# VectorE's dependent chains issued in turns, two products moved ahead, and v centred without an fp32 matmul, in a cross-attention and mixture-of-experts kernel

## The reference, cut to what matters

```python
x = x + xattn(layernorm(x), ctx, ctx, igate_w, igate_b, fgate_w, fgate_b, out_w)
x = x + ffn(layernorm(x), gate_w, w1, b1, w2, b2)
# x, ctx: (32, 128, 256); 8 heads of 32
# xattn: gates i, f of [q, k, v];  log_f = log_sigmoid(f);  cs = cumsum(log_f)
#   D = exp(cs_s - cs_t + i_t - max over t <= s);  C = (q k^T / sqrt(32)) * D
#   h = C v / (max(|sum C|, exp(-max)) + 1e-6);  each head of h is normed (mean, variance), times out_w
# ffn: softmax gates over 8 experts, the best two of each token, gelu MLP 256 -> 1024 -> 256, weighted sum
```

## Time and profile before

| | |
|---|---|
| times of three runs | 648.76, 648.89, 652.68 us; median 648.89 |
| the profiled execution | 651.1 us, its span 649.1 us (2.0 us lie around the span) |
| busy in the span | PE 611.4 (94%), PEld 526.6, DVE 487.2 (75%), ACT 323.4 (50%), POOL 193.7 us |
| first steps | 0 to 102.55 us |
| the five bodies on DVE | 29.01, 27.40, 27.40, 27.39 and 30.04 us long |
| the expert tiles behind | from 243.79 us on, PE busy 395.13 of 396.21 us to 640 |

### The profile page before, as it was taken

One profiled execution on the slowest core, in us unless ns is written; L12 is line 12 of the kernel. 1 busy time (PEld: TensorE's weight loads), 2 busy tenths in 40 slices (PEclk: granted clock), 3 DMA queues, 4 the chain that ended last, 5 costly groups with the idle time before them and its releaser, 6 DMA issues. The chain is left out here.

```text
span 649.1 us, 20273 instructions
## 1 busy us (share of the span) xinstructions
PE 611.4 (94%) x6736; PEld 526.6 (81%) x6737; DVE 487.2 (75%) x1330; ACT 323.4 (50%) x767; POOL 193.7 (30%) x185
## 2 busy tenths in 40 slices
PE   1799999999999899999999999999999999999995
PEld 1567777777777668998988988888989888989994
DVE  2546988999999898995888967666676757575684
ACT  2677888897988747544432323233232323232341
POOL 3000002242433424235345523232222323232333
PEclk9898998999999999999999999999999999999998
DMA  4443635475655626233464432323132323243510
GB/s 143 134 127 118 209 99 187 147 238 194 220 166 142 198 91 231 70 73 92 75 186 108 70 68 38 65 36 65 33 62 33 66 33 66 67 119 81 141 34 2
DMA packets 56044, 70.22 MB, mean 108 GB/s; under 512 B 5584, under 2 KB 50832, under 8 KB 55840
## 3 DMA queue, kind: packets, MB, share of 16 engines
q1 hardware_dynamic: 42560, 51.80, 26.3%
q0 software_dynamic: 13296, 17.32, 14.7%
q10 hardware_dynamic: 112, 0.08, 0.0%
HBM read 41.50 MB, written 24.92 MB: 102 GB/s over the span
## 5 line engine op out<-in xcount | busy, mean ns | idle before, releaser
L1059 ACT ACTIVATE decay_slots<-scores,b_turned 128x256 f32<-128x256 f32 (+1 forms) x312 | 124.4, 451 | 241.2 <-PE scores L1545 235.1
L1545 PE MATMUL scores<-x_slots,w_halves 128*128 128x256 f16 (+1 forms) x1760 | 193.7, 266 | 0.0
L1545 PEld LDWEIGHTS scores<-x_slots,w_halves 128*128 x1760 | 165.2, 98 | 17.3
L662 POOL DMA_INDIRECT expert_rows<-xf_rows,slot_i x64 | 71.9, 1124 | 211.8 <-issue 107.0
L1559 PE MATMUL pv<-w_halves,decay_slots 128*128 x864 | 97.6, 273 | 0.0
L684 POOL DMA_INDIRECT out_rows<-v_centred_and_one,row_ids x36 | 58.3, 1619 | 129.2 <-DVE v_centred_and_one L2146 95.7
L1559 PE MATMUL gate_bank<-w_halves,q_and_k_halves 128*128 x840 | 95.0, 273 | 0.0
L1559 PEld LDWEIGHTS pv<-w_halves,decay_slots 128*128 128x128 f16 x864 | 84.4, 98 | 9.7
L1559 PEld LDWEIGHTS gate_bank<-w_halves,q_and_k_halves 128*128 128x128 f16 x840 | 82.0, 98 | 9.5
L684 POOL DMA_INDIRECT out_rows<-work,row_ids x35 | 56.2, 1605 | 104.6 <-DVE work L2146 82.6
L1278 PEld LDWEIGHTS pv<-v_centred_and_one,decay_slots 128*128 128x128 f32 x512 | 63.7, 194 | 1.6
(11 more groups left out here) (263 smaller groups left out, 864.5 us busy)
## 6 DMA issues: line engine op xcount, KB each, us to landing
weight_stage<-in_L_ffn_w SPq DMA_DIRECT2D x32, 512.0 KB, 4.0
x_slots<-in_x SPq DMA_DIRECT2D x16, 512.0 KB, 4.4
weight_stage<-expert_rows SPq DMA_DIRECT2D x30, 272.0 KB, 3.2
ctx_slots<-in_ctx SPq DMA_DIRECT2D x8, 512.0 KB, 6.0
out_rows<-x_slots SPq DMA_DIRECT2D x8, 512.0 KB
v_centred_and_one<-expert_rows SPq DMA_DIRECT2D x9, 272.0 KB, 3.0
expert_rows<-v_centred_and_one SPq DMA_DIRECT2D x9, 272.0 KB, 3.2
xf_rows<-w_halves SPq DMA_DIRECT2D x4, 512.0 KB, 4.1
```

What stands on the lines that cost most here:

```text
L662: pool.indirect_dma_start(table, bass.IndirectOffsetOnAxis(ap=sloti[:, step[1], j, k:k + 1], axis=0), xfn[:, step[1], j, :], None, bounds_ ...
L1059: ins = act.activation(hf[:, f * R:f * R + tr.rows(0)], ps_s[:, q, n * R:n * R + tr.rows(0)], ACT.Gelu, bias=b1T[:, bass.ds(expert, 1), f] ...
L1545: ins = pe.matmul(o, w, xh[:, tr.slot(0) % 2, b, k, 0:tr.rows(0)], start=(n == 0), stop=(n == 3 * KC - 1))
```

## The change

- **In turns.** Each DVE chain becomes a generator: an instruction that the next one depends on is followed by `yield`, and the wait for it is written ahead of the next. `go_on(chain)` takes one piece, `whole(chain)` all of it. The body calls pieces of two chains alternately: `next_norm` with `next_a`, `split` with `h_norm`, `h_scaled` and `gate_bias` with `choose`, `x1_stats` with `records`. In the first steps and in the tail all chains are taken whole.
- **Moved.** On DVE `c_of(step, 2)` goes ahead of `x1_norm(last)`, and `c_of(step, 3)` ahead of the BN_AGGR. On PE `times_v(step, 3)` goes from behind `turn(after, 1)` to ahead of `xf_left(last, 0)`, with one `stream` ahead of it, and the three ahead of `times_v(step, 2)` become one. ACT's order follows.
- **v centred.** The weight matrix now holds 1 - 1/32 on its diagonal and -1/32 in the rest of a head's block. So the four f16 products of a row give v minus its mean, and the fp32 product with the identity that gave v itself is gone. POOL makes the matrix with one more `affine_select`.

```diff
-        meanw = sb("minus_mean_of_head", [P, P], F16)
+        centring = sb("one_minus_mean_of_head", [P, P], F16)
...
+                pool.wait_ge(s_mean, 2)
+                pool.affine_select(out=centring[:, :], in_=centring[:, :], compare_op=ALU.not_equal,
+                                   fill=1.0 - 1.0 / DH, base=0, pattern=[[-1, P]],
+                                   channel_multiplier=1).then_inc(s_cp, 1)
...
@@ centre (PE)
-                        pe.matmul(ps_h[:, n * D:n * D + D], ident[:, :], ctxb[:, j, :], start=True, stop=False)
                         for c in range(KC):
                             for a in range(2):
                                 ins = pe.matmul(ps_h[:, n * D + c * P:n * D + c * P + P], qkT[:, step[1], j, a, KC + c, :],
-                                                meanw[:, :], start=False, stop=(c == KC - 1 and a == 1))
+                                                centring[:, :], start=(c == 0 and a == 0),
+                                                stop=(c == KC - 1 and a == 1))
...
@@ refine (DVE), as all chains
-                    c.link(dve, dve.tensor_tensor(t, y, y, ALU.mult))
+                    c.inc(dve.tensor_tensor(t, y, y, ALU.mult))
+                    yield
+                    c.wait(dve)
...
@@ body (PE)
                         scores(step, 3)
-                        turn_xf(last, 0)
                         log_f_sum(nxt)
-                        stream_before(step, 2, 3)
+                        stream_before(step, 2, 1)
                         times_v(step, 2)
+                        turn_xf(last, 0)
+                        stream_before(step, 3, 1)
+                        times_v(step, 3)
                         xf_left(last, 0)
                         turn(after, 0)
                         turn_a(nxt)
                         turn(after, 1)
-                        times_v(step, 3)
...
@@ body (ACT)
-                        x1_normed(last, 0)
-                        x1_normed(last, 1)
                         h_out(step, 1)
                         decay(step, 3, 1)
+                        x1_normed(last, 0)
+                        x1_normed(last, 1)
+                        weights_high(nxt, 1)
                         x1_normed(last, 2)
-                        xf_turned(last, 0)
+                        h_out(step, 2)
                         next_guess(after)
-                        weights_high(nxt, 1)
+                        xf_turned(last, 0)
+                        x1_normed(last, 3)
                         next_normed(after, 0)
                         next_normed(after, 1)
-                        h_out(step, 2)
+                        h_out(step, 3)
                         next_normed(after, 2)
                         next_normed(after, 3)
                         xf_low(last, 0)
                         turned(after, 0)
                         turned(after, 1)
-                        x1_normed(last, 3)
-                        h_out(step, 3)
```

More of the change, by code:

```diff
@@ L872, in body @@
                         turned(after, 1)
-                    if last is not None:
-                        x1_normed(last, 3)
-                    if step is not None:
-                        h_out(step, 3)
-                    if after is not None:
                         q_low(after, 0)
@@ L1916, in body @@
                 def body(last, step, nxt, after):
+                    nothing = iter(())
+                    incoming, scaling = (next_stats(after), next_norm(after)) if after is not None else (nothing,) * 2
+                    sums, bias = (next_a(nxt) if nxt is not None else nothing,
+                                  gate_bias(after) if after is not None else nothing)
+                    parted = split(nxt) if nxt is not None else nothing
+                    norm, scaled = (h_norm(step), h_scaled(step)) if step is not None else (nothing,) * 2
@@ L1917, in body @@
+                    choice, record = (choose(last), records(last)) if last is not None else (nothing,) * 2
+                    outgoing = x1_stats(step) if step is not None else nothing
+                    if step is not None:
+                        c_of(step, 2)
                     if last is not None:
                         x1_norm(last)
+                    for _ in range(SB):
+                        go_on(incoming)
                     if step is not None:
-                        c_of(step, 2)
@@ L1921, in body @@
-                    if after is not None:
-                        next_stats(after)
+                        c_of(step, 3)
+                    go_on(incoming)
+                    go_on(incoming)
                     if nxt is not None:
                         weights_low(nxt, 0)
-                    if after is not None:
-                        next_norm(after)
-                    if step is not None:
-                        c_of(step, 3)
+                    go_on(scaling)
+                    go_on(sums)
@@ L1934, in body @@
+                    go_on(parted)
+                    go_on(norm)
+                    go_on(parted)
+                    go_on(norm)
+                    if nxt is not None:
                         max_log_decay(nxt)
-                    if step is not None:
-                        h_norm(step)
+                    go_on(norm)
                     if nxt is not None:
                         weights_low(nxt, 2)
+                    go_on(norm)
+                    go_on(choice)
+                    go_on(choice)
@@ L1939, in body @@
+                    go_on(scaled)
+                    go_on(choice)
+                    go_on(scaled)
+                    go_on(choice)
+                    go_on(scaled)
+                    go_on(choice)
+                    go_on(scaled)
+                    go_on(choice)
                     if step is not None:
-                        h_scaled(step)
                         h_weighted(step)
-                    if last is not None:
-                        choose(last)
-                    if after is not None:
-                        gate_bias(after)
+                    go_on(choice)
@@ L1958, in body @@
                         c_of(nxt, 2)
-                    if step is not None:
-                        x1_stats(step)
-                    if last is not None:
-                        records(last)
+                    go_on(outgoing)
+                    go_on(record)
+                    go_on(outgoing)
+                    go_on(record)
+                    go_on(outgoing)
+                    go_on(record)
+                    go_on(outgoing)
+                    go_on(record)
+                    go_on(outgoing)
+                    go_on(outgoing)
                 def first_steps():
-                    next_stats(S0)
-                    next_norm(S0)
+                    whole(next_stats(S0))
+                    whole(next_norm(S0))
                     weights_low(S0, 0)
@@ L2182, in _ @@
                 split_rows(Turn(0, 0), 0)
[L2183 removed]
+                whole(h_norm(last))
                 split_rows(Turn(0, 0), 1)
                 row_fields(Turn(0, 0), 1)
[L2186 removed]
+                whole(h_scaled(last))
                 h_weighted(last)
```

215 lines of the change are left out of this document (141 added, 74 removed).

## The result

The changed kernel takes **674.81 us** (median of 4 runs, 670.9 to 680.74) against 650.7 us for the kernel before on the same chip: a ratio of **1.0385, 95% interval 1.0327 to 1.0442**. The forecast was 656.5 us, 647 to 663. Slower was right; the size was not.

What follows compares the result with a forecast made beforehand. The prediction took DVE to bound the bodies at 27.40 us. First steps -1.0, first body +0.1, bodies 2 to 4 +6.75, fifth -0.3 and clock +2.1 made +7.65 on 648.9: 656.5 us, range 647 to 663.

Steps and rivals of the forecast that it cites:

- middle bodies: Bodies 2 to 4: 29.65 us each, 2.25 more than now, with 0.7 us each for the clock on top.
- (a): DVE at the body's head: the q scale starts at 7.0 us instead of 4.90, behind more large instructions.
- (d): Further waits: late `x1_guess` and decay put the q scale at 7.55 us; DVE's waits sum to 6.4 us a body.
- the clock's 0.7: Bodies 2 to 4: PE's 1.8 us gap ahead of `q_left` lowers its clock, costing 0.7 us each, between 0 and 1.7.
- (c): DVE from the start of `choose` to the next body: 11.45 us instead of 10.80, so a body takes at least 28.05.
- links saved a body: DVE: some 34 dependent pairs a body, each 0.12 us shorter in turns, 4 us less of DVE's own work.
- fifth body: Last body: waits of 2.0 us for `turn_a` and 1.1 at `choose` against some 3.5 of links, -0.3 us.
- the one on v centred: PE without the fp32 product: a gain of 1.0 us in the first steps, bounds 0 and 7.4; 0 in the bodies.
- The 669 us of that rival: Rival: turns save nothing on DVE, 13.9 us behind `choose`, bodies of 32 us, 669 us in all; chance 0.03.
- The waits did not overlap to 28.05 us: Rival: waits overlap and the body stays near its floor of 28.05 us, 648.6 to 653 in all; chance 0.30.
- DVE was held by the logits: Denies the faster rival: DVE not held by the logits, a body about 25 us, 635.5 in all; chance 0.08.
- the last rival's 6.8 us: Rival: the clock costs its upper end in four bodies, 6.8 us instead of 2.1, 661 to 666 in all; chance 0.04.

Runs made afterwards that it cites:

- after_fp32: The changed kernel with the fp32 product of the centring put back, all else as changed: 662.66 us, ratio 1.0222 to the kernel before.
- centre_only: The kernel before with only the new centring matrix and the fp32 product gone: 661.94 us, ratio 1.0142 to the kernel before.
- three_places_back: The changed kernel with the fp32 product back and three DVE places restored (h scaling before choose, earlier q scale, x1's variance before records): 651.75 us, ratio 1.0014.
- after_streams_first: The changed kernel, without the fp32 product, with four filler products ahead of each centring call of the first four steps alone: 662.91 us, ratio 1.0183.
- gap_filled: The changed kernel with the fp32 product back and six filler products in PE's gap ahead of `q_left`: 661.11 us, ratio 1.0172.
- choose_behind: The changed kernel with the fp32 product back and `h_scaled` and `h_weighted` whole ahead of the rest of `choose` on DVE: 659.34 us.
- var_x_ahead: The changed kernel with the fp32 product back and `x1_stats` finished ahead of `records` on DVE: 661.34 us.
- q_scale_ahead: The changed kernel with the fp32 product back and the last link of `next_norm` ahead of the second `weights_low` on DVE: 654.52 us.
- careful_turns: The kernel before with DVE turns only where nothing that waits is put ahead, and one wait less in `records`: 652.85 us, ratio 1.0025.

## Why the prediction was wrong in the first steps, and nearly right in the middle bodies

Its steps, against the profile after. "Body" is a middle one.

| step | forecast | measured |
|---|---|---|
| q scale, from the body's start (a) | 7.55 us | 7.56 |
| `running_max` ready for its wait, and the wait (d) | 7.6, 1.5 | 7.7, 1.49 |
| `max_log_decay`, third `weights_low`: waits (d) | 0.5, 1.0 | 0.59, 1.30 |
| `choose` starts, with the clock's 0.7 | 18.9 | 19.06, after a wait of 2.85 |
| from there to the next body (c) | 11.45 | 11.57 |
| PE's gap ahead of `q_left`, clock behind it, bodies 2 to 4 | 1.8, some 0.5 | 1.78, 0.57 |
| clock behind that gap, first body | lowered, as before | 1.00 |
| middle bodies, each against 27.40 | +2.95 | +3.24, +3.23, +3.33 |
| links saved a body | 4.0 | 3.2 |
| v centred, in a middle body | 0 | -0.4 (against after_fp32) |
| first body | +0.1 | +0.62 |
| fifth body | -0.3 | +1.96 |
| first steps | -1.0 | **+6.5** |
| behind the bodies | 0 | +0.7 |

**The failed step is the one on v centred**, "In the first steps it counts where PE leads ... That is 0.9 to 1.0". The sum took the fp32 product as time that PE gives back. The gain it priced did come, 0.6 us at the c product of 38.67. But the runs showed the product's occupation of PE to be what held the clock: with nothing else changed the first body starts 7.1 us later without it (centre_only), and in the order of after 8.5 us later than with it (after_fp32). The prediction did price the clock, but only for the gap that it made itself in the bodies, by the earlier trace rows; it didn't ask the same of the work it took away, though both its bounds, 0 and 7.4 us, were on the side of a gain. The profiles differ by 12.0 us more than forecast (19.6 against 7.65), and 7.5 of them are this term; an end at a loss of such a size would have taken the range past 663. The median misses by 6.3 us more (18.3): 3.9 of that because the other runs of after are longer than the profiled one and had lower mean clocks, 2.2 because the forecast went to a median lower than its profile. What those longer runs lost is in no profile.

**The fifth body** is the second, 2.3 us. Its two waits were foreseen as 2.0 and 1.1 and measured 2.06 and 1.86; a third, for `decay(3, 1)` ahead of the fourth c product, was not in the sum:

```profile
233.25 1.22 DVE L1779 SCALAR_TENSOR_TENSOR decay_slots<-scores,decay_slots 128x1024 f32<-128x1024 f32 x1 [1.30 <-ACT decay_slots L793]
239.06 0.29 DVE L1723 COPY a_and_running_max<-gate_bank 96x128 f32<-96x128 f32 x1 [2.06 <-PE gate_bank L1204]
...
245.86 0.19 DVE L1856 TENSOR_REDUCE top<-route_bank 128x4 f32<-128x32 f32 x1 [1.86 <-PE route_bank L1307]
```

With 0.51 us for ACT's `rstd_x` at its end, DVE waits 5.73 us in this body, where before it waited 1.23; its own work fell from 28.81 to 26.27, by 2.5 us and not by 3.5. 4.50 - 2.54 = 1.96 is the whole difference.

**The middle bodies** held: the mechanism was laid out wait by wait, and came out 0.3 us too short each. Inside the sum two errors offset in part: DVE's own work was 24.0 us where 23.25 was forecast, its waits 6.63 where they were 7.1 (6.4 and 0.7 for the clock). And v centred, put at nothing here, gave 0.4. That the loss is in the places and not in the turns is shown by three_places_back. The clock's share, taken as 0.7 us a body, was 0.7 by the bodies of after_streams_first that kept the full clock (29.90 against 30.64 in after), and 1.05 in gap_filled (with the fp32 product). But the gap alone does not decide: the first body of after had it too, at a clock of 1.00. Of the rule on waits between dependent instructions that was weighed against the trace ("VectorE: DVE Perf Modes" of the Trainium skill, section "The DRAIN you can't avoid"; its half on counting ops and not semaphores stands under "Rules for kernel authors"), the trace after says again that short dependent instructions do cost by their waits: 24.0 against 27.2 us of own work for the same instructions. The 669 us of that rival lie nearer to the result by accident: it had 13.9 us behind the start of `choose` and bodies of 32 us, where 11.57 and 30.6 were measured, and nothing in the first steps.

**The rivals.** The waits did not overlap to 28.05 us; DVE was held by the logits; and the clock did cost more than the last rival's 6.8 us, but in the first steps, where that rival had not placed it.

## What to carry to other kernels

Before taking work off an engine that isn't the bound, look at the granted clock around it: here 1.8 us a step less took the stretch from 40 to 60 us from 0.91 to 0.66, and the whole program behind it came 6.5 us later, though the same edit had first brought it 0.6 us forward. When a chain is issued in turns with another, write down for each piece what it waits for and who is queued behind it; one link behind a 1.1 us instruction (the q scale) was worth 1.9 us a body, more than half of what all the links saved (3.2). And when DVE, PE and ACT are all within 2 to 4 us of the body, a saving on one can come back as a wait on the next: here 0.9 us less on DVE and 1.1 less on PE left the body at 27.5. And where the clock takes two values in bodies of one kernel, compare bodies at the same clock: choose_behind and var_x_ahead each had one body that looked like a gain of 1.3 to 1.6 us and was mostly the clock.

## What the runs showed of the hardware

- Filler products nobody reads were worth as much as the fp32 product: 662.5 and 662.66 us, both with a clock of 1.00 from 40 to 60 us, against 0.66 without either (0.91 in the kernel before).
- In bodies 2 to 4 of after a gap of PE of 1.78 us came with a stretch of 3.8 us at a clock of 0.57 to 0.59; with 1.3 us of filler in it, a gap of 0.47 us and a clock of 1.00. "TensorE: Matmul & The Clock Gate" of the Trainium skill, section "HAM oscillation — how this bites in real kernels", tells of this: a wait between bursts of matmuls puts the clock down again in each pass. These bodies agree, with a wait of 1.78 us. But the same gap stood at a clock of 1.00 in the first body of after and in every other body of after_streams_first, and one of 1.5 us in all four bodies of q_scale_ahead. What else decides is open.
- What the two levels cost one and the same body: 31.51 us at a mean clock of 0.89 and 29.90 at 1.00 in after_streams_first, with the same gap of 1.79 us.
- In the first body of careful_turns PE waited 2.04 us for a transfer of ctx, where before it was 1.21. The clock was 0.67, 0.50 and 0.80 in the three windows of 5 us from 106 us on, and the body took 32.67 us instead of 29.01:

```profile
108.58 0.66 PE L1142 MATMUL scores<-ident,x_slots 128*128 128x128 f32 x2 [2.04 <-DMA ctx_slots<-in_ctx]
```
